# Attention with relation bias and a mixture of experts: copied relation maps, longer loop turns, moved maximum matmuls, alternating expert products

## The reference, cut to what matters

```python
x = x + attn(layernorm(x))
x = x + ffn(layernorm(x))
# attn:
scores = einsum(q, k) / sqrt(hd)
logits = li[:, None] + lj[None, :] + rel_b               # per query and key, 3 relations
probs = softmax(logits)                                  # the relation maps
bias = einsum('bijk,hk->bhij', probs, logical_bias)
out = softmax(scores + gate * bias) @ v @ Wo.T + bo
# ffn: top 2 of 8 experts per token
h = relu(x @ W1[e] + b1[e]); y = h @ W2[e] + b2[e]; sum of the two, weighted
```

## Time and profile before

| | us |
|---|---|
| median of 3 runs (lowest to highest) | 5311.16 (5309.63 to 5318.84) |
| profiled execution, device time | 5305.37 |
| its span, first to last instruction | 5303.6 |
| PE busy | 4609.0 (87%) |
| DVE busy | 4010.2 (76%) |
| ACT busy | 3394.0 (64%) |
| POOL busy | 2102.8 (40%) |
| mean granted TensorE clock | 0.932 of full |

### The profile page before, as it was taken

How to read it: one execution, slowest core, us unless ns; L and a number is a source line. 1 busy time by engine, 2 the same in 40 slices (tenths; PEclk the granted TensorE clock), 3 DMA queues, 4 the chain that set the end, 5 groups by cost and what they waited for, 6 DMA issues and landing times. The chain is left out here.

```text
span 5303.6 us, 184408 instructions
## 1 busy us (share of the span) xinstructions
PE 4609.0 (87%) x74128; PEld 3497.3 (66%) x74128; DVE 4010.2 (76%) x6341; ACT 3394.0 (64%) x4457; POOL 2102.8 (40%) x1811
## 2 busy tenths in 40 slices
PE   4548999999999999999999999999999983688882
PEld 3216777777777777777777777777777773466662
DVE  7288888888888888888888888888888613566663
ACT  0136877878787878787787878787878840233330
POOL 4043444444444444444444444444444413323234
PEclk8758999999999999999999999999999985789996
DMA  2634555555555555555555555555555552333323
GB/s 58 101 95 119 150 137 151 149 139 150 141 149 145 150 137 148 142 146 137 151 151 138 151 142 150 144 151 136 148 140 147 143 161 89 115 115 116 113 105 107
DMA packets 455013, 710.53 MB, mean 134 GB/s; under 512 B 138664, under 2 KB 306472, under 8 KB 425792
## 3 DMA queue, kind: packets, MB, share of 16 engines
q1 hardware_dynamic: 447936, 681.00, 47.0%
q0 software_dynamic: 6144, 16.79, 1.0%
HBM read 506.30 MB, written 184.93 MB: 130 GB/s over the span
## 5 line engine op out<-in xcount | busy, mean ns | idle before, releaser
L685 DVE TENSOR_REDUCE b_mxp<-b_mx 128x1 f32<-128x512 f32 x4096 | 2624.7, 683 | 541.0 <-PE b_mx L786 466.3
L653 ACT ACTIVATE b_pr<-b_sc 128x1024 f32<-128x1024 f32 x2048 | 1987.7, 1021 | 773.1 <-PE b_sc L775 772.5
L764 PE MATMUL b_sc<-b_qm,kst 128*128 128x128 f16 x16384 | 1276.4, 221 | 86.6 <-issue 82.0
L775 PE MATMUL b_sc<-b_cm,b_rst 112*128 112x128 f16 x16384 | 1275.8, 221 | 1.3 <-issue 1.3
L764 PEld LDWEIGHTS b_sc<-b_qm,kst 128*128 128x128 f16 x16384 | 977.8, 98 | 284.8 <-ACT b_pr L653 174.0
L775 PEld LDWEIGHTS b_sc<-b_cm,b_rst 112*128 112x128 f16 x16384 | 976.0, 98 | 227.7 <-issue 227.6
L811 PE MATMUL b_acc<-b_pr,vp 128*32 128x128 f32 x32768 | 1110.9, 276 | 0.5 <-issue 0.5
L811 PEld LDWEIGHTS b_acc<-b_pr,vp 128*32 128x32 f32 x32768 | 835.3, 110 | 231.6 <-ACT b_pr L653 195.4
L594 POOL CAST b_rhi<-b_ex 128x512 f16<-128x512 f32 x512 | 321.4, 628 | 1570.5 <-ACT b_ex L639 785.7
L786 PE MATMUL b_mx<-kst,b_qx 64*128 64x512 f16 x4096 | 822.8, 398 | 120.8 <-DVE b_mxp L685 116.0
L590 POOL TENSOR_TENSOR b_ex<-b_ex 128x512 f32<-128x512 f32 x512 | 658.0, 1285 | 528.7 <-ACT b_ex L631 528.1
(11 more groups left out here) (143 smaller groups left out, 2016.8 us busy)
## 6 DMA issues: line engine op xcount, KB each, us to landing
b_dj<-key_logits SPq DMA_DIRECT2D x256, 768.0 KB, 7.5
b_rst<-relation_parts SPq DMA_DIRECT2D x256, 512.0 KB, 4.8
relation_parts<-b_rhi SPq DMA_DIRECT2D x512, 128.0 KB
relation_parts<-b_rlo SPq DMA_DIRECT2D x512, 128.0 KB
b_rst<-relation_parts SPq DMA_DIRECT2D x256, 256.0 KB, 5.3
c_w1r<-in_L_ffn_W_dram SPq DMA_DIRECT2D x23, 1024.0 KB, 4.8
c_w2r<-in_L_ffn_W_dram SPq DMA_DIRECT2D x23, 1024.0 KB, 4.8
expert_tokens<-c_zeros SPq DMA_DIRECT2D x23, 512.0 KB, 7.0
```

What stands on the lines that cost most here:

```text
L653: nc.scalar.activation(pr[:, jt % 2, half, :], sc[:, half].rearrange("p a b -> p (a b)"), ACT.Exp).then_inc(s["p_ready"], 1)
L685: nc.vector.tensor_reduce(mxp[:, head, part:part + 1], mx[:, (bank + ab) % MX_RING, :], AX.X, ALU.max).then_inc(s["mx_used"], 1)
L764: pe.matmul(sc[:, half, side, p * P:p * P + P], kst[:, pair, jt * P:jt * P + P], qm[:, par, pair, :, side * IS:side * IS + IS], start=(p = ...
L775: ins = pe.matmul(out, rst[:, u % 2, b, j0:j0 + P], cm[:, par, half, b], start=False, stop=(b % (NB // 2) == NB // 2 - 1), skip_group_chec ...
```

## The change

1. `in_chunks`: ten chunks in the loop body and three turns; chunks 30 and 31 stay behind the loop.
2. Relation maps: no DRAM tensor. `sp_r` copies each group straight from `rhi`/`rlo` (now 4 slots) to `rst`, six DMAs of 64 KB for a group. The maps of chunk c are now made two units ahead (`R_AHEAD` = 4 groups) and not a chunk ahead, the last chunk included. POOL waits for the copies of two units before (`r_in`) and not for writes to DRAM. The queries of a block are now i = 64 side + 4 q + part, so the bias matmuls write with a stride of 4 elements.
3. VectorE: the clamp stands behind the second pair of reductions, and `dve_acc` stands in step 31 between its two pairs.
4. TensorE: the order in one step is S C S C P V P.
5. `sp_m` issues 2 DMAs and not 8; the stores to `c_dram` are 6 DMAs and not 48, with the same 32-byte pieces; `sp_consts` moves to the end of a chunk; `sp_dj` loads four units ahead.
6. Experts: TensorE alternates two up tiles of block b with one down tile of block b-1. VectorE follows with two splits and one bias, and `split_x` stands behind the splits of f = 4, 5. ScalarE converts the weights after f = 1 and f = 3, not 3 and 5.

```diff
+R_AHEAD, D_AHEAD = 4, 3
+CLAMP_SLOT, ACC_SLOT = 1, 0
+UNROLL, LOOPS = 10, 3
...
-    with eng.Fori(0, (NT - 2) // 2) as pair:
-        chunk(pair * 2, 0, pair + 1, False)
-        chunk(pair * 2 + 1, 1, pair + 1, False)
-    chunk(NT - 2, 0, NT // 2, False)
-    chunk(NT - 1, 1, NT // 2, True)
+    with eng.Fori(0, LOOPS) as turn:
+        for n in range(UNROLL):
+            chunk(turn * UNROLL + n, n % 2, turn * (UNROLL // 2) + n // 2 + 1, False)
+    for c in range(LOOPS * UNROLL, NT):
+        chunk(c, c % 2, c // 2 + 1, c == NT - 1)
...
-                    for b in range(NB):
-                        sp.dma_start(c_dram[:, part, k].rearrange("x (i b) h -> b i x h", b=NB)[b],
-                                     t[BI * b:BI * b + BI, k]).then_inc(stored, 16)
+                    sp.dma_start(c_dram[:, part, k].rearrange("x p h -> p x h"), t[:, k]).then_inc(stored, 16)
...
+        def sp_r(sp, x, u, k):
+
+            sp.wait_ge(s["lo_ready"], 16 * x + 2 * u + k + 1)
             waited(sp)
+            for side in range(2):
+                for part, t in enumerate((rhi, rlo, rhi)):
+                    row = 32 * part + BI * k
+                    sp.dma_start(rst[row:row + BI, u % 2, NB // 2 * side:NB // 2 * side + NB // 2, :],
+                                 t[IS * side:IS * side + IS, 2 * (u % 2) + k, :]).then_inc(s[f"r_in{u % 2}"], 16)
...
+                    sp.wait_ge(s["scores_ready"], STEPS * c + max(SPU * u, 1))
+                    waited(sp)
                     for k in range(2):
+                        if u + 1 < UNITS:
+                            sp_r(sp, c, u + 1, k)
                         elif not last:
+                            sp_r(sp, c + 1, 0, k)
                         if u == 0 and k == 0 and not last:
                             sp_q(sp, c + 1, 1 - par)
                         if u == M_UNIT and k == 0 and not last:
                             sp_m(sp, c + 1, 1 - par)
+                    if u + 4 < UNITS or not last:
+                        sp.wait_ge(s["d_ready"], 32 * c + 4 * u + 12)
+                        waited(sp)
+                        sp_dj(sp, (u + 4) % UNITS)
...
+                    g = jt // 2 + R_AHEAD
+                    if g < 2 * UNITS:
+                        (act_r_inv if jt % 2 else act_r_exp)(act, c, g)
+                    elif not last:
+                        (act_r_inv if jt % 2 else act_r_exp)(act, c + 1, g - 2 * UNITS)
...
-                if n % 3 == 0 and n // 3 < 2 * UNITS:
+                if n % 2 == 0 and n < 2 * R_AHEAD:
                     for k in range(2):
-                        dve_d(dve, 0, 0, 1, n // 3, k)
+                        dve_d(dve, 0, 0, 1, n // 2, k)
...
+                        if slot == CLAMP_SLOT:
+                            g, k = R_AHEAD + (jt + D_AHEAD) // 2, (jt + D_AHEAD) % 2
+                            if g < 2 * UNITS:
+                                dve_d(dve, c, par, nth, g, k)
+                            elif not last:
+                                dve_d(dve, c + 1, 1 - par, nth + par, g - 2 * UNITS, k)
...
-                side, i0 = b // (NB // 2), b % (NB // 2) * BI
-                out = sc[:, half, side, :].rearrange("p (h i) -> p h i", h=HH)[:, :, i0:i0 + BI]
+                side, part = b // (NB // 2), b % (NB // 2)
+                out = sc[:, half, side, :].rearrange("p (h i b) -> p h i b", h=HH, b=NB // 2)[:, :, :, part]
...
-                        pe_scores(pe, c, par, jt + 1, 0, first_pair)
-                        pe_scores(pe, c, par, jt + 1, 1, lambda: None)
+                        for half in range(2):
+                            pe_scores(pe, c, par, jt + 1, half)
...
+                    pe_step_pair(pe, c, par, nth, jt, 0, last, more)
+                    pe_pv(pe, c, jt)
                     pe_step_pair(pe, c, par, nth, jt, 1, last, more)
-                    pe_pv(pe, c, jt)
...
+                for i in range(BT):
+                    if b < NBLK:
+                        if i == 0:
+                            pe.wait_ge(s["w1_lo"], b + 1)
+                            pe.wait_ge(s["x_lo"], KC * (b + 1))
+                        for f in range(i * FT // BT, (i + 1) * FT // BT):
+                            up(pe, b, f)
+                    if b + 1 < NBLK and i == 1:
+                        turn_x(pe, b + 1)
+                    if b > 0:
+                        if i == 0:
+                            pe.wait_ge(s["w2_lo"], b)
+                            pe.wait_ge(s["h_split"], 2 * FT * b)
+                        down(pe, b - 1, i)
```

More of the change, by code:

```diff
@@ L513, in sp_m @@
             waited(sp)
-            for b in range(NB):
-                sp.dma_start(cval[M_ROW:M_ROW + BI, par, b], m16[BI * b:BI * b + BI, :]).then_inc(s["m_in"], 16)
+            for side in range(2):
+                sp.dma_start(cval[M_ROW:M_ROW + BI, par, NB // 2 * side:NB // 2 * side + NB // 2, :],
+                             m16[IS * side:IS * side + IS, :]).then_inc(s["m_in"], 16)
         @block.sync
@@ L528, in _ @@
             sp.dma_start(att_dram[0], att[:, :, :].rearrange("p h w -> p (h w)")).then_inc(s["att_out"], 16)
[L529 to L533, removed]
+            for u in range(2, 4):
+                sp.wait_ge(s["d_ready"], 4 * (u - 1))
+                sp_dj(sp, u)
+            for k in range(2):
+                sp_r(sp, 0, 0, k)
             sp_m(sp, 0, 0)
@@ L565, in chunk @@
                             sp_qx(sp, c + 2, par)
-                            sp_consts(sp, c + 2, par)
+                    if u + 1 == UNITS and more:
+                        sp_consts(sp, c + 2, par)
             in_chunks(sp, chunk)
@@ L608, in _ @@
             pool.wait_ge(s["eye_made"], ROWS // BI + 1)
-            for g in range(2 * UNITS):
+            for g in range(R_AHEAD):
                 pool_r(pool, 0, g)
@@ L614, in chunk, with act_r_exp @@
             def chunk(c, par, nth, last):
-                if not last:
-                    for g in range(2 * UNITS):
-                        pool_r(pool, c + 1, g)
-                        if g in C_MAPS:
-                            pool_c(pool, c + 1, 1 - par, nth + par, C_MAPS.index(g))
+                for turn in range(2 * UNITS):
+                    g = turn + R_AHEAD
+                    if g < 2 * UNITS:
+                        pool_r(pool, c, g)
+                    elif not last:
+                        pool_r(pool, c + 1, g - 2 * UNITS)
+                    if turn in C_MAPS and not last:
+                        pool_c(pool, c + 1, 1 - par, nth + par, C_MAPS.index(turn))
             in_chunks(pool, chunk)
-        def act_r_exp(act, x, u, k):
-            g = 16 * x + 2 * u + k
+        def act_r_exp(act, x, n):
+            g, k = 16 * x + n, n % 2
             act.wait_ge(s["d_ready"], 2 * g + 2)
@@ L643, in _ @@
             nc.scalar.preload_act_table_set("natural_log_exp_and_others")
-            for u in range(UNITS):
-                for k in range(2):
-                    act_r_exp(act, 0, u, k)
-                    act_r_inv(act, 0, u, k)
+            for g in range(R_AHEAD):
+                act_r_exp(act, 0, g)
+                act_r_inv(act, 0, g)
             def chunk(c, par, nth, last):
@@ L725, in _ @@
                 dve_pair(dve, 1, n, 2 * PAIRN + 2 * n)
-            for k in range(2):
-                dve_d(dve, 1, 1, 1, 0, k)
+            for n in range(D_AHEAD):
+                dve_d(dve, 0, 0, 1, R_AHEAD + n // 2, n % 2)
             def chunk(c, par, nth, last):
@@ L1290, in turn_x, with up, down @@
                 ins.then_inc(s["x_turned"], 1)
+        parts = ((0, 0), (1, 0), (0, 1))
+        def up(pe, b, f):
+            n = b * FT + f
+            if n >= 4:
+                pe.wait_ge(s["relu_done"], n - 3)
+            for c in range(KC):
+                for wp, xp in parts:
+                    ins = pe.matmul(ps[:, n % 4, :], w1p[:, b % 2, wp, c, f:F:FT], xT[:, b % 2, xp, c],
+                                    start=(c == 0 and wp == 0 and xp == 0), stop=(c == KC - 1 and xp == 1))
+            ins.then_inc(s["up_done"], 1)
+        def down(pe, b, t):
+            d = BT * b + t
+            if d >= 2:
+                pe.wait_ge(s["y_done"], d - 1)
+            for f in range(FT):
+                for hp, wp in parts:
+                    ins = pe.matmul(ps[:, 4 + d % 2, 0:D], hT[:, b % 2, hp, f, t * P:t * P + P],
+                                    w2p[:, b % 2, wp, f, :], start=(f == 0 and hp == 0 and wp == 0),
+                                    stop=(f == FT - 1 and wp == 1))
+            ins.then_inc(s["down_done"], 1)
         @block.tensor
```

184 lines of the change are left out of this document (59 added, 125 removed).

## The result

| | before | after |
|---|---|---|
| median of 4 runs (lowest to highest), us | 5312.39 (5309.63 to 5318.84) | 5762.83 (5761.73 to 5765.87) |
| span of the profiled execution, us | 5303.6 | 5762.0 |
| mean granted TensorE clock | 0.932 | 0.957 |

The ratio is 1.0847, 95% interval 1.0828 to 1.0866: the changed kernel is slower by 8.5%, where 4945 us and a range of 4890 to 5060 had been predicted.

A forecast was written before the change was run, and what follows sets the result against it. TensorE was taken to set the attention's pace, with VectorE's late biases stalling it in the experts. Savings 96 + 98 + 16 + 17 - 7 + 145 = 365 from 5305 gave 4940, stated as 4945 us, range 4890 to 5060.

The forecast's parts named there:

- Relation maps within SBUF: Attention's relation maps copied without DRAM: cost 0, bound 0 to 31 us; bias output stride also 0, bound up to 98.
- C: Rival, slower: SP can't issue the relation copies fast enough, at 1.24 us each; 5508 us, chance 0.05.
- Loop returns: Attention loop: 12 fewer returns at 8.0 us each save 96 us, bounds 72 to 110.
- Order of the step: TensorE's attention step: four shape changes instead of five, 3.55 by the pieces, 3.56 taken against 3.66, saving 98 us.
- Rival D: Attention step: the new order gives nothing because V to P costs two changes; 5043 us, sharing chance 0.25.
- Rival A: Attention: VectorE's clamp meets POOL's subtraction, so the second P waits every second step; 5240 us, chance 0.07 in full.
- Clamps of 0.9 to 1.1: Sign to look for on VectorE in the attention: clamps take 0.9 to 1.1 us and not 0.5.
- Relation copies: SP's six copies for unit 6's second group, behind the maxima's: landed by 14.5, wanted at 14.7, so just in time.
- Head and projections: Before the first step: fewer clamps and key-logit waits save 16 us, earlier query stores in the projections 17.
- Last chunk: Last attention chunk now makes its own relation maps, ScalarE needing 3.2 against TensorE's 2.92 for 24 steps: 7 us lost.
- Experts: Expert stage: 22 blocks go from 29.0 to 22.4 us each, saving 145 us, bounds 88 to 163.
- rival B: Expert blocks stay bound by VectorE at 25 us each, 57 us later in all; 5002 us, sharing chance 0.25.

The follow-up runs named there:

- b_stride: The kernel before with only the bias matmul's output changed to single columns four apart (exponentials of half the score): 6112.85 us against 5309.05, ratio 1.1517.
- a_runs2: The changed kernel with bias outputs in pairs of neighbouring columns, eight apart, and exponentials of half the score: 4955.61 us, one execution.
- e_runs: The changed kernel with bias outputs back in runs of 16 neighbouring columns, using 12 more small constant DMAs a chunk: 5101.92 us, ratio to before 0.9609.
- d_runs_m: e_runs with the eight maxima copies behind the unit's twelve relation copies and the map products half a unit later: 4974.56 us, ratio to before 0.9373.
- d_loop2: d_runs_m with two chunks a loop turn (15 turns) instead of ten (3 turns): 5055.25 us, ratio to before 0.9529.
- a_runs4: The changed kernel with bias outputs in runs of four neighbouring columns, 16 apart, and exponentials of half the score: 4958.59 us, one execution.
- d_order: d_runs_m with the step order of before on TensorE, and VectorE's clamp and accumulator read back in their old places: 5046.90 us, ratio to before 0.9509.
- b_experts: The kernel before with only the changed kernel's expert stage: 5159.11 us against 5305.34, ratio to before 0.9719.

## Why the prediction was wrong

**The step that failed** is in "Relation maps within SBUF": "The stride of the bias output has no row; the same elements are written, so I take 0, bounds from nothing to 0.1 a step (98)". A step has 16 bias matmuls, and each went from 56 to 109 ns, 0.85 in all. `b_stride` gives it as +804 us in the old kernel. In the changed one it is 5762.83 - 4955.61 = 807, with the one execution of `a_runs2`.

The reason given, that the same elements are written, doesn't hold: their number didn't change, and the time doubled. The bound was eight times too low, because it was not made from a row at all. It was a guess at a small effect; a doubling of the two groups, 1024 x 2 x 0.45 = 922, would have covered it. The text ahead of the prediction names the stride of 4 elements, but misread the layout of before. It says that block b of `rst` holds the queries 8 q + b; that is their order in the DRAM tensor, and the block holds 16 neighbouring ones, which is why its output came in runs of 16. So the change was from runs of 16 to single columns, in instructions of the engine that sets the pace.

None of the four rivals was this one. C, the slower one, had SP as its mechanism, and the copies took 0.59 as forecast, not 1.24. So the chance of 0.05 for slower rested on the wrong place. The prediction's own test held: "wrong above all if the step is longer than 3.66".

**Loop returns**, 96 predicted, 81 measured. The mechanism was right; 6.7 a return lies under the 8.0 taken and inside the bounds.

**Order of the step**: 3.55 by the pieces, 3.553 measured in `e_runs`, `d_runs_m`, `d_loop2`, `a_runs2` and `a_runs4`. Rival D is false. The term of 98 came to 72 after the stops above.

**Rival A** did not come, as `d_runs_m` shows at the short step: TensorE's waits for the reductions are 82, not one in every second step.

```profile
PE b_mx L782 <- DVE b_mxp L681: 83.1, 82, 15.3
```

Clamps of 0.9 to 1.1 had been forecast. The mean is 682 ns, against 756 before and 803 in `d_order`, so the new order made it shorter. POOL does hold the clamp up: in `before`, `d_runs_m` and `d_order` every clamp of over 0.6 us (434, 462 and 542 of 1024) ends 0.28 after the end of an instruction of POOL. In `d_runs_m` that is the sum in 447 cases, as the prediction had it, and hardly ever the subtraction.

```profile
L673 DVE TENSOR_SCALAR b_dl<-b_dj,b_const 128x512 f32<-128x512 f32 x1024 | 696.6, 682 | 55.6 <-DMA b_dj<-key_logits 33.8 <-ACT b_ex L629 21.6
```

**Relation copies**: "just in time" was right in unit 6. In the changed kernel `sp_m` is two copies and TensorE has no wait for `b_rst`, but its step is 4.41. At the short step `a_runs2`, also with two copies, waits 1.1 us in all; `e_runs`, with eight, waited 93. What the move into SBUF is worth by itself wasn't measured.

**Head and projections**: 33 predicted, 14.8 measured. Six stores in place of 48 cost SP 17.0 and not the 3 implied, since each takes 2.7 to 3.0 in the mean where the 48 took 0.54 each: the issue is paid mostly by the small pieces and not by the DMA, which was the lower bound's condition. SP was free at 145.19, not 131, and VectorE's wait fell by 6.3 and not 17. That leaves 8.5 for the head, where 16 had been taken; why wasn't traced. TensorE's first scores start at 410.0, not near 390.

**Last chunk**: 7 lost predicted, 4 measured (88.7 to 92.6 from its first V to its last, in `d_runs_m`).

**Experts**: 145 predicted, 146 measured alone (`b_experts`); rival B is false. That the two agree so closely is luck. The working has 3.2 less 2.6 as 0.1 at the seam, where it is 0.6, so by its own terms a block takes 22.9. A block took 21.92, with no wait at the seam, and only 20 of the 22 periods came down from 29.0, which gives 141.

The sum with the right price of the stride would have been 4945 + 807 = 5752, against 5762.83. That is the same as saying that 4945 is 11 below the 4955.61 of `a_runs2`. It is 30 below the 4974.56 of `d_runs_m`, which has 12 more DMAs a chunk. Part of this closeness is luck too. Undone one at a time, loop and order came out 15 and 26 smaller than their terms, and head and projections 18. Against that, TensorE's waits for VectorE at P, which the sum left alone, went from 116.0 to 83.1 in `d_runs_m`.

## What to carry to other kernels

When a change of layout lets a DMA do less, look at who then reads or writes the other order, and count that engine's instructions. Here 16 matmuls in each of 1024 steps, on the engine that sets the pace, paid for DMAs that were already hidden. If an order has to be turned, turn it where an element is at least a pair, or in small loads outside the inner loop, as `e_runs` does for 12 DMAs a chunk.

A diff that keeps an operation's count and size but changes its access pattern has no row in the old trace. Its upper bound should be a multiple of the instruction, not a small fraction of the step.

## What the runs showed of the hardware

- At a granted clock of 0.98 to 1.00 (the 2.4 GHz level), a matmul of 128 columns took 56 ns with outputs in runs of 2, 4 or 16 f32 columns, and 109 ns with single columns two or four apart. With four apart it took 109 ns whether it added to the bank or started a sum.
- The moving operand does the same: single f16 columns four apart took 110 ns, pairs of them four apart 57. The Trainium skill, SBUF — State Buffer, in the section named above, has SBUF in lines of 16 bytes, with full rate from two hits in a line. Single f16 columns four apart lie eight bytes apart and hit each line twice, so by that rule they are free; the 110 ns say otherwise for a matmul.
- A store of 32-byte pieces held its queue 2.7 to 3.0 us in the mean for one DMA, so eight times fewer DMAs with the same pieces saved 8.8 us of 25.8.
- A clamp on VectorE took 0.48 us alone. Each one that took over 0.6 ended 0.28 after an instruction of POOL: 434, 462 and 542 times in `before`, `d_runs_m` and `d_order`, without exception.
- TensorE stopped for up to 3.0 us within a group of matmuls, for nothing that the profile shows, 36 times at V in `d_runs_m` and 11 times in `d_order` with its longer step. The stops come back at the same places of the loop body (38 of 42 at four places in `d_loop2`). The cause stays open.
